# First feed-forward layer of a cross-attention block by seven block products, and its output projection on f16 halves

## The chip, the cores and the metric
One Trainium2 chip, one of its cores. The metric is the device time of one execution in microseconds (us). The core has five engines with queues in program order: TensorE (PE, with its weight loads PEld), VectorE (DVE), ScalarE (ACT), GpSimd (POOL) and SyncE (SP), which issues the DMAs. They wait for each other by semaphores.

## The reference, cut to what matters
16 sequences of 512 rows and 512 features, 16 heads, 2048 hidden features.
```python
q, k, v = (split_heads(t @ W + b) for t, W, b in ((x, Wq, bq), (ctx, Wk, bk), (ctx, Wv, bv)))
attn = softmax(where(j < i, q @ k.T / sqrt(32), -1e30)); attn[row 0] = 0
x = layer_norm(x + (attn @ v) @ Wo + bo, g1, be1)
out = layer_norm(x + relu(x @ W1 + b1) @ W2 + b2, g2, be2)
```

## The kernel before, in words
Every product is made in halves: a number is split into a high and a low half (f16, or f32r in the projection), and three matmuls (high high, high low, low high) stand for one of f32.

`attention` runs 16 sequences in windows of 48 slots. Beside it, `Bounds` scans W2 and then W1 for their largest entries, one tile of 128x1024 in each sequence; for W2 (sequences 0 to 7) GpSimd also makes five sums of quarters, and three DMAs store seven blocks, so that the second layer needs seven block products instead of eight.

`feed` takes over at the end of the attention: 32 chunks of 256 tokens in windows of 16 slots. It is interleaved with the attention's last slots (`side_by_side`), up to about its slot 20. `due(window, s, ..., first, span)` gives the item whose step `first` falls in this slot: a chunk's steps are spread over some 48 slots, and three chunks overlap. Each engine's program goes through the slots in order; within one slot the order is that of the text. No barrier stands between slots: only semaphores hold the engines together. Slot numbers of the steady state are taken modulo 16.

A chunk's steps in `feed`: the context and x are loaded (`LOAD`), the context is turned in 32x32 blocks on DVE (`OTR`), split into halves (`turned`), multiplied by Wo (`PROJ`, slots 5 and 6, two PSUM banks `front`), added to x and normed (`RES`, `NORM1`), stored and loaded turned (`x1_rows`, `X1_TURN` 13), split (`x1_halves`). The first layer (`FFN1` 16, one block of 128 hidden features a slot) writes `h_ps`, ScalarE makes `hf` of it, GpSimd sums, ScalarE and DVE the halves `hs`. The second layer (`FFN2` 22, two slots for one pair) adds seven products in `acc`, four PSUM banks, which the next chunk needs one slot after the last product. DVE reads them out in slots `RES2 - 1` (four parts) and `RES2` (two), then norms (`STATS2`, `NORM2`). Weight chunks go through `raw`: ScalarE makes the high half, DVE the low half, 44 chunks and Wo's four.

## Time and profile before
| | us |
|---|---|
| median of three runs (2651.48 to 2652.87) | 2652.14 |
| profiled execution, its own time | 2651.14 |
| its span, first to last instruction | 2649.3 |
| TensorE busy (94%) | 2498.2 |
| VectorE busy (80%) | 2116.9 |
| ScalarE busy (62%) | 1629.8 |
| GpSimd busy (60%) | 1585.5 |

The granted TensorE clock is 0.989 of full speed over the span. Busy shares are means over the attention (to some 1120 us), the handover and the feed-forward part, whose limits differ; they are read by stage. A matmul's own duration holds its way through the pipeline, so what it costs in a stream is read from start to start.

### The profile page before, as it was taken

To read this page: it belongs to the slowest core of one execution; us is meant where nothing else is said; L and a number is where in the kernel's file an instruction comes from. 1 tells how busy PE (TensorE), PEld (TensorE's weight loads), DVE (VectorE), ACT (ScalarE), POOL (GpSimd) and SP (SyncE) were. 2 spreads that over 40 slices of the span, in tenths; PEclk is the share of its full clock that TensorE was granted. 3 is DMA by queue.
4 is the path that set the end of the run, shared out by engine and by line. 5 is a ranking of instruction groups with operands and counts; after the bars stand their busy time and mean duration, and the time that the engine had idled before them with its cause. 6 is when DMAs were issued, how large, how long until landed. Compare 5 with 4: busy or idle time off the path is not lost.

```text
span 2649.3 us, 62863 instructions
## 1 busy us (share of the span) xinstructions
PE 2498.2 (94%) x22664; PEld 1873.3 (71%) x22664; DVE 2116.9 (80%) x4886; ACT 1629.8 (62%) x2881; POOL 1585.5 (60%) x1721
## 2 busy tenths in 40 slices
PE   4899999999999999879999999999999999999998
PEld 1455555555555555557888888888888888888887
DVE  7999999999999999878767777767767676767675
ACT  2788889899899999886344444343444343444433
POOL 2677777777777777666455555555555555554543
PEclk9999999999999999989999999999999999999999
DMA  5344444443344443345232313222222222222220
GB/s 169 110 117 117 119 114 110 115 109 103 92 103 105 106 106 97 89 140 159 53 69 50 71 46 67 50 69 53 66 56 61 61 57 64 57 65 57 65 57 25
DMA packets 444456, 225.04 MB, mean 85 GB/s; under 512 B 302368, under 2 KB 388192, under 8 KB 444144
## 3 DMA queue, kind: packets, MB, share of 16 engines
q1 hardware_dynamic: 442544, 219.71, 32.5%
q8 instruction: 179, 2.93, 0.5%
q10 hardware_dynamic: 1600, 1.31, 0.2%
q14 instruction: 133, 1.09, 0.1%
HBM read 112.36 MB, written 57.69 MB: 64 GB/s over the span
## 4 chain that ended last, share of the span: by engine, by line
PE 63%; DVE 8%; SPq 8%; POOL 8%; issue 7%; DMA 4%; ACT 1%; ACTq 0%; DVEq 0%; POOLq 0%
PE h_ps L1646 23%; PE acc L1662 20%; POOL prob_lo L495 7%; PE front L1632 6%; PE lin_ps L934 5%; SPq L421 4%; PE max_ps L907 2%; PE st_ps L955 2%; DVE max_ps L886 2%; PE lin_ps L930 1%; PE o_ps L973 1%; SPq L458 1%; SPq L1065 1%; DMA heads<-stage 1%; PE st_ps L986 1%
## 5 line engine op out<-in xcount | busy, mean ns | idle before, releaser
L495 POOL TENSOR_TENSOR prob_lo<-probs,prob_hi 128x512 f16<-128x512 f32 (+1 forms) x768 | 797.8, 1047 | 335.2 <-ACT prob_hi L582 318.5
L1646 PE MATMUL h_ps<-x_halves,W 128*128 128x256 f16 x6144 | 756.2, 273 | 1.8 <-ACT hf L1431 1.7
L1662 PE MATMUL acc<-W,hs 128*128 128x256 f16 x5376 | 669.6, 273 | 0.3 <-DVE hs L1599 0.3
L1646 PEld LDWEIGHTS h_ps<-x_halves,W 128*128 128x128 f16 x6144 | 596.5, 98 | 87.5 <-issue 14.8
L1431 ACT ACTIVATE hf<-h_ps,b1s,scale_evac 128x256 f32<-128x256 f32 x512 | 284.9, 563 | 559.7 <-PE h_ps L1646 557.2
L1662 PEld LDWEIGHTS acc<-W,hs 128*128 128x128 f16 x5376 | 526.0, 98 | 61.4 <-DVE hs L1599 0.6
L1356 POOL TENSOR_TENSOR hf<-hf 128x256 f32<-128x256 f32 x256 | 243.4, 951 | 483.1 <-ACT hf L1431 482.7
L588 ACT ACTIVATE probs<-st_ps,exp_scale 128x512 f32<-128x512 f32 (+1 forms) x768 | 469.3, 611 | 98.2 <-PE st_ps L986 91.6
L886 DVE CUSTOM_DVE_ANT_0 max_ps<-max_ps,mask_q 128x256 f32<-128x256 f32 (+2 forms) x768 | 418.2, 560 | 47.1 <-PE max_ps L907 43.4
L582 ACT ACTIVATE prob_hi<-probs 128x512 f16<-128x512 f32 (+1 forms) x768 | 427.9, 557 | 23.0 <-issue 7.3
L1599 DVE TENSOR_TENSOR hs<-hf,hs 128x896 f16<-128x896 f32 x256 | 282.0, 1121 | 147.8 <-ACT hs L1420 147.7
L1420 ACT ACTIVATE hs<-hf 128x896 f16<-128x896 f32 x256 | 242.0, 945 | 252.8 <-POOL hf L1359 248.4
L907 PE MATMUL max_ps<-heads 96*128 96x128 f16 (+3 forms) x1024 | 258.1, 303 | 74.9 <-DVE maxima L886 62.9
L955 PE MATMUL st_ps<-heads 98*128 98x512 f16 (+3 forms) x1024 | 268.4, 303 | 14.3 <-DMA heads<-rows 11.0
L973 PE MATMUL o_ps<-V,prob_hi 128*128 128x65 f16 x2560 | 247.6, 191 | 9.5 <-DVE onorm L807 4.7
L907 PEld LDWEIGHTS max_ps<-heads 96*128 96x128 f16 x1024 | 89.8, 97 | 231.0 <-DVE maxima L886 100.5
L975 PE MATMUL o_ps<-V,prob_lo 128*128 128x33 f16 x2560 | 237.6, 179 | 0.0
L973 PEld LDWEIGHTS o_ps<-V,prob_hi 128*128 128x128 f16 x2560 | 200.5, 97 | 51.0 <-issue 10.4
L930 PE MATMUL lin_ps<-wv,acts 128*128 128x512 f16 x768 | 209.5, 383 | 26.9 <-DVE acts L596 26.8
L1357 POOL TENSOR_TENSOR hf<-hf 128x256 f32<-128x256 f32 x256 | 229.3, 896 | 0.0
L934 PE MATMUL lin_ps<-acts,wk 128*128 128x512 f16 x768 | 208.6, 381 | 5.4 <-DVE V L853 5.4
L934 PE MATMUL lin_ps<-acts,wq 128*128 128x512 f16 x768 | 207.6, 380 | 3.2 <-DVE V L853 3.2
(152 smaller groups left out, 3526.1 us busy)
## 6 DMA issues: line engine op xcount, KB each, us to landing
heads<-stage SPq DMA_DIRECT2D x748, 64.0 KB, 2.1
raw_c<-in_cT SPq DMA_DIRECT2D x64, 256.0 KB, 3.4
raw_x<-in_xT SPq DMA_DIRECT2D x64, 256.0 KB, 4.4
o_in<-ctx_rows SPq DMA_DIRECT2D x256, 64.0 KB, 2.5
x_in<-in_x SPq DMA_DIRECT2D x32, 512.0 KB, 4.0
x_rows<-x SPq DMA_DIRECT2D x64, 256.0 KB, 2.1
o_in<-x_rows SPq DMA_DIRECT2D x256, 64.0 KB, 2.4
out<-y SPq DMA_DIRECT2D x32, 512.0 KB, 3.0
```

What stands on the lines that cost most here:

```text
L495: pool.tensor_tensor(prob_lo[:, k % 4, 0:w], probs[:, k % PROBS, 0:w], prob_hi[:, k % 4, 0:w], ALU.subtract).then_inc(pl_done, 1)
L582: act.activation(prob_hi[:, k % 4, 0:w], probs[:, k % PROBS, 0:w], ACT.Copy).then_inc(ph_done, 1)
L588: act.activation(probs[:, k % PROBS, 0:w], st_ps[:, k % 2, 0:w], ACT.Exp, bias=PROB_BIAS, scale=exp_scale[:, at:at + 1]).then_inc(exp_done, 1)
L886: last = dve.tensor_tensor_reduce(out=scores[:, a, :], in0=scores[:, a, :], in1=mask_q[:, S - w:S], scale=1.0, scalar=MASKED, op0=ALU.add, ...
L907: last = pe.matmul(max_ps[:, bank, a * w:(a + 1) * w], heads[t][0:96, 0, i, q * P:(q + 1) * P], heads[t][0:96, 1, i, 0:w], start=(a == 0), ...
L934: last = pe.matmul(lin_ps[:, n % 2, :], W[kind][:, aw, j, t * P:(t + 1) * P], act_part(item, side, aa)[:, j, :], start=(j == 0 and m == 0) ...
L955: pe.matmul(st_ps[:, k % 2, at:at + w], heads[t][0:98, 1, i, kt * P:(kt + 1) * P], heads[t][0:98, 0, i, kt * P:S], start=(m == 0), stop=False,
L973: pe.matmul(o[:, 0:2 * HD + 1], prob_hi[:, k % 4, col:col + P], v[:, 0:2 * HD + 1], start=(k % 3 == 0 and q == 0), stop=False, skip_group_ ...
L1431: act.activation(to, h_ps[:, f % 2, 0:T].rearrange("p (u n) -> p u n", u=U), ACT.Relu, bias=b1s[:, f:f + 1], scale=h_evac).then_inc(h_out, 1)
L1599: dve.tensor_tensor(hs[:, p % HS, 1, :, :], hf[:, (PAIRS * item.n + p) % HF, 1:1 + PRODUCTS, :], hs[:, p % HS, 0, :, :], ALU.subtract).the ...
L1646: last = pe.matmul(h_ps[:, f % 2, 0:T], W1[:, aw, j, f * P:(f + 1) * P], x1_halves[:, item.parity, aa, j, :], start=(j == 0 and m == 0), s ...
L1662: last = pe.matmul(acc_products[:, n, :], hs[:, p % HS, aa, n, :], W2[:, p, aw, n, :], start=(p == 0 and m == 0 and n % 2 == 0), stop=(p = ...
```

## The change
The first layer is done for four blocks of hidden features (two pairs) at a time, in four stages with seven products together. x1 and W1 are cut in quarters; W1's sums are made by GpSimd in sequences 8 to 15, as W2's were before them, and stored to `mixed_w1`; x1's sums are made by GpSimd in each chunk (`X1_MIX`), after which ScalarE and DVE split seven blocks of x1 instead of four. Partial sums stay in PSUM (`mix_b`, `mix_ad`) and are drawn out between the stages: ScalarE copies M2 and U2 to `sums`, DVE adds C11, C22 and C21, ScalarE applies the ReLU. `first_product` waits for C11 before stage 1, for U2 before stage 2 and for C22 before stage 3.

`FFN1` goes to slot 18, `FFN2` to 30 (14 in the window), `PROJ` to slots 4 and 6 with one PSUM bank, so that the second projection waits for the first residual; `RES2 - 1`, `RES2` and `STATS2` fall on slots 13, 14 and 15. x1 is loaded back into `y` from DRAM instead of being kept. Wo and the context are split into f16 halves; Wo is loaded and scanned early in the attention (`load_wo`). W1 now has 28 chunks, so there are 56 of W1 and W2, and Wo's four. The order within a slot on ScalarE is: last quadrant (`C12_AT`), ReLUs, x1 high halves, context high half, weights, roots, `H_HI`, M2, U2; on DVE: C11, C22, C21, x1 low halves, turns, context low half, residual and first norm, reads of `acc`, second norm, `H_LO`, weights.

```diff
+        quarter = scan[:, 0:2, :].rearrange("p i (j e n) -> p (i j) e n", j=2, e=2)
+        a11, a12, a21, a22 = (quarter[:, 2 * i:2 * i + 2, e, :] for e, i in ((0, 0), (0, 1), (1, 0), (1, 1)))
+        s1, s2, s4 = (scan[:, 2 + n // 2, 256 * (n % 2):256 * (n % 2) + 256].rearrange("p (j n) -> p j n", j=2)
+                      for n in range(3))
+        return [(s1, a21, ALU.add, a22), (s2, s1, ALU.subtract, a11), (s4, a12, ALU.subtract, s2),
+                (a21, a11, ALU.subtract, a21)]
...
-                    for n, src in enumerate(bounds.tiles(item.n)):
+                    for n, (dst, src) in enumerate(bounds.tiles(item.n, scan)):
                         wait_for(sp, bounds.kept, 1, item, 0)
-                        if item.n <= bounds.pairs:
-                            wait_for(sp, bounds.mix_stored, 48, item, 0)
-                        sp.dma_start(scan[:, n, :], src).then_inc(bounds.loaded[n], 16)
+                        wait_for(sp, bounds.mix_stored, 48, item, 0)
+                        sp.dma_start(dst, src).then_inc(bounds.loaded[n], 16)
                 for item, _ in due(window, s, SLOTS, B, MIX_STORE):
...
+                for n in range(5):
                     for item, _ in due(window, s, SLOTS, B, MIX + 3 * n):
-                        if item.n >= bounds.pairs:
+                        mixes = bounds.mixes(item.n, scan)
+                        if n >= len(mixes):
                             continue
...
+                        if item.n >= bounds.pairs and n:
+                            pool.wait_ge(bounds.mixed, bounds.mixed_by(item.n) + n)
+                        elif n >= 3:
+                            pool.wait_ge(bounds.mixed, bounds.mixed_by(item.n) + 3)
+                        out, in0, op, in1 = mixes[n]
+                        pool.tensor_tensor(out, in0, in1, op).then_inc(bounds.mixed, 1)
...
+    BV_AT = 3
     OTR = 2
+    ADD_BO = 3
+    PROJ = (4, 6)
+    RES = (5, 7)
     NORM1 = 8
     X1_TURN = 13
+    X1_MIX = (X1_TURN + 2, X1_TURN + 4)
+    X1_HI = (X1_TURN + 3, X1_TURN + 5)
+    X1_LO = (X1_TURN + 4, X1_TURN + 6)
+    FFN1 = 18
+    STAGES = (0, 2, 3, 5)
+    M2_AT = FFN1
+    C11_AT, U2_AT, C22_AT, C21_AT, C12_AT = FFN1 + 1, FFN1 + 2, FFN1 + 4, FFN1 + 6, FFN1 + 6
+    RELU = FFN1 + 7
+    MIX = FFN1 + 8
+    H_HI = FFN1 + 9
+    H_LO = FFN1 + 10
+    FFN2 = FFN1 + 12
+    Y_LOAD = 40
+    ADD_B2 = 43
     RES2 = FFN2 + FT
+    STATS2 = RES2 + 1
     NORM2 = RES2 + 8
     STORE = RES2 + 9
+    SPLIT = 4
     RAW = early.RAW
     PAIRS = FT // 2
+    TWOS = PAIRS // 2
     PRODUCTS = 7
     HALVES = ((0, 1, 2, 3), (4, 5, 6))
+    STEPS = ((("b", 1, 1), ("a", 0, 0), ("d", 2, 2)), (("a", 5, 5),), (("a", 4, 4),), (("a", 6, 3), ("d", 3, 6)))
...
+    def region(name, two):
+
+
+        if name == "b":
+            return mix_b[:, 0:2, :]
+        return mix_ad[:, two % 2, {"a": 0, "d": 2}[name]:{"a": 2, "d": 4}[name], :]
...
+                for half in range(2):
+                    for item in x1_items(window, s, X1_MIX[half]):
+                        for n, (to, in0, in1) in enumerate((((4, 2, 0), (2, 3, 2)), ((5, 3, 4), (6, 1, 5)))[half]):
+                            if (half, n) == (0, 0):
+                                wait_for(pool, x1_turned, U, item, U)
+                                wait_for(pool, x1_lo, 2, item, 0)
+                                pool.wait_ge(bv_done, 1)
+                            else:
+                                wait_for(pool, x1_mixed, 4, item, 2 * half + n)
+                            pool.tensor_tensor(blocks[:, to, :], blocks[:, in0, :], blocks[:, in1, :], ALU.subtract
+                                               ).then_inc(x1_mixed, 1)
...
+                for item, k in when(window, s, C12_AT, FT):
+                    two, r = k // 4, k % 4
+                    if r < 2:
+                        p = 2 * two + r
...
+                        wait_for(act, c21_done, TWOS, item, two + 1)
+                        wait_for(act, h_lo, PAIRS, item, p + 1 - HF)
+                        act.activation(hf[:, (PAIRS * item.n + p) % HF, 8, :], region("a", two)[:, r, :], ACT.Relu,
+                                       bias=b1s[:, 2 * p:2 * p + 1], scale=h_evac).then_inc(h_last, 1)
+                for item, k in when(window, s, RELU, FT):
+                    two, r = k // 4, k % 4
+                    if r < 2:
+                        p = 2 * two + r
+                        h, c = hf[:, (PAIRS * item.n + p) % HF, :, :], sums[:, two % 2, r, :, :]
+                        wait_for(act, c21_done, TWOS, item, two + 1)
+                        wait_for(act, c22_done, TWOS, item, two + 1)
+                        for to, odd in ((slice(2, 3), 0), (slice(0, 2), 1)):
+                            act.activation(h[:, to, :], c[:, to, :], ACT.Relu, bias=b1s[:, 2 * p + odd:2 * p + odd + 1],
+                                           scale=h_evac).then_inc(h_out, 1)
+                for half in range(2):
+                    for item in x1_items(window, s, X1_HI[half]):
+                        part = X1_PARTS[half]
+                        wait_for(act, x1_mixed, 4, item, 2 * half + 2)
+
+                        wait_for(act, stage_done[3], TWOS, item, -TWOS)
+                        act.activation(x1_halves[:, item.parity, 0, part, :, :],
+                                       blocks[:, part, :].rearrange("p m (j n) -> p m j n", j=2), ACT.Copy,
+                                       scale=scale_x1).then_inc(x1_hi, 1)
...
+                for item, k in when(window, s, M2_AT, FT):
+                    if k % 4 == 0:
+                        two = k // 4
...
+                        wait_for(act, m2_done, TWOS, item, two + 1)
+                        wait_for(act, h_out, FT, item, 4 * two - 4)
+                        act.activation(sums[:, two % 2, :, 2, :], region("b", two), ACT.Copy).then_inc(m2_kept, 1)
+                for item, k in when(window, s, U2_AT, FT):
+                    if k % 4 == 0:
+                        two = k // 4
+                        wait_for(act, stage_done[1], TWOS, item, two + 1)
+                        act.activation(sums[:, two % 2, :, 0:2, :].rearrange("p r c n -> p c r n"),
+                                       mix_ad[:, two % 2, :, :].rearrange("p (c r) n -> p c r n", c=2), ACT.Copy
+                                       ).then_inc(u2_kept, 1)
...
+                for item, k in when(window, s, C11_AT, FT):
+                    if k % 4 == 0:
+                        two = k // 4
+                        wait_for(dve, stage_done[0], TWOS, item, two + 1)
+                        wait_for(dve, m2_kept, TWOS, item, two + 1)
+                        dve.tensor_tensor(sums[:, two % 2, :, 2, :], sums[:, two % 2, :, 2, :], region("a", two), ALU.add
+                                          ).then_inc(c11_done, 1)
+                for item, k in when(window, s, C22_AT, FT):
+                    if k % 4 == 0:
+                        two = k // 4
+                        wait_for(dve, stage_done[2], TWOS, item, two + 1)
+                        wait_for(dve, u2_kept, TWOS, item, two + 1)
+                        dve.tensor_tensor(sums[:, two % 2, :, 1, :], sums[:, two % 2, :, 1, :], region("a", two), ALU.add
+                                          ).then_inc(c22_done, 1)
+                for item, k in when(window, s, C21_AT, FT):
+                    if k % 4 == 0:
+                        two = k // 4
+                        wait_for(dve, stage_done[3], TWOS, item, two + 1)
+                        dve.tensor_tensor(sums[:, two % 2, :, 0, :], sums[:, two % 2, :, 0, :], region("d", two), ALU.add
+                                          ).then_inc(c21_done, 1)
...
-                        dve.scalar_tensor_tensor(out=tile, in0=front[:, u, :],
+                        dve.scalar_tensor_tensor(out=tile, in0=front[:, :],
...
+        def first_product(item, two, stage):
+
+            if stage == 0:
+                wait_for(pe, x1_lo, 2, item, 1)
...
+                wait_for(pe, h_last, PAIRS, item, 2 * two + 2 - 4)
+                wait_for(pe, c21_done, TWOS, item, two + 1 - 2)
+                wait_for(pe, m2_kept, TWOS, item, two)
+            elif stage == 1:
+                wait_for(pe, x1_lo, 2, item, 2)
+                wait_for(pe, c11_done, TWOS, item, two + 1)
+            elif stage == 2:
+                wait_for(pe, u2_kept, TWOS, item, two + 1)
+            else:
+                wait_for(pe, c22_done, TWOS, item, two + 1)
+            for name, at_w, at_x in STEPS[stage]:
+                for r in range(2):
+                    for j in range(2):
+                        for m, (aw, aa) in enumerate(((0, 0), (0, 1), (1, 0))):
+                            opens = stage == 0 and name != "d" and r == 0 and j == 0 and m == 0
+                            last = pe.matmul(region(name, two)[:, r, :], w1_of(2 * two + r, aw, at_w)[:, j, :],
+                                             x1_halves[:, item.parity, aa, at_x, j, :], start=opens,
+                                             stop=(j == 1 and m == 2), skip_group_check=True)
+                if name == "b":
+                    last.then_inc(m2_done, 1)
+            last.then_inc(stage_done[stage], 1)
...
+        def first_products(window, s):
+
+            for stage, at in enumerate(STAGES):
+                for item, k in when(window, s, FFN1 + at, FT):
+                    if k % 4 == 0:
+                        first_product(item, k // 4, stage)
...
+                    for item, _ in when(window, s, PROJ[u]):
+                        wait_for(pe, ctx_lo, U, item, u + 1)
+                        wait_for(pe, res_done, U, item, u)
                         if item.n == 0:
-                            pe.wait_ge(w_lo, KT)
+                            pe.wait_ge(wo_lo, KT)
+                            pe.wait_ge(*before.lin_read)
                         for j in range(KT):
                             for m, (aa, aw) in enumerate(((0, 0), (0, 1), (1, 0))):
-                                last = pe.matmul(front[:, u, :], turned[:, item.parity, aa, j, u * P:(u + 1) * P],
+                                last = pe.matmul(front[:, :], turned[:, item.parity, aa, j, u * P:(u + 1) * P],
                                                  Wo[:, aw, j, :], start=(j == 0 and m == 0),
...
+                if s % 2 == 0:
+                    first_products(window, s)
+                    second_products(window, s)
+                else:
+                    second_products(window, s)
+                    first_products(window, s)
```

## Rows read from the trace of the kernel before

**Rows 1.** Busy time by stage: us, PE, PEld, DVE, ACT, POOL, clock, DMA.
```profile
1209.00:1257.00 48.00, 44.43 (x370) 38.05 (x369) 43.01 (x56) 31.98 (x52) 29.22 (x29) 0.96 0.53 143
1257.00:2557.60 1300.60, 1300.23 (x11130) 1142.39 (x11129) 924.03 (x1508) 535.23 (x870) 674.30 (x811) 1.00 0.26 60
2557.60:2634.00 76.40, 76.40 (x675) 67.70 (x674) 48.52 (x77) 32.04 (x51) 34.89 (x50) 1.00 0.10 29
```

**Rows 2.** Order of time, TensorE: the projections of chunks 2 and 31.
```profile
1256.95 3.01 PE L1632 MATMUL front<-Wo,turned 128*128 128x512 f32 x12
...
2558.41 2.99 PE L1632 MATMUL front<-Wo,turned 128*128 128x512 f32 x12
```

**Rows 3.** Order of time, a steady chunk: start, us, instructions.
```profile
1808.74 1.47 PE L1646 MATMUL h_ps<-x_halves,W 128*128 128x256 f16 x12
...
1810.05 1.47 PE L1662 MATMUL acc<-W,hs 128*128 128x256 f16 x12
```

**Rows 4.** The same: a projection and what follows it.
```profile
1800.96 3.02 PE L1632 MATMUL front<-Wo,turned 128*128 128x512 f32 x12
...
1803.82 1.21 PEld L1646 LDWEIGHTS h_ps<-x_halves,W 128*128 128x128 f16 x12 [0.26 <-issue]
```

**Rows 5.** Order of time in the attention, TensorE.
```profile
800.22 0.38 PE L907 MATMUL max_ps<-heads 96*128 96x128 f16 x4 [1.03 <-DVE maxima L886]
800.44 0.38 PE L911 MATMUL max_ps<-mask_q,identb 128*128 128x512 bf16 x1
...
800.99 0.19 PE L973 MATMUL o_ps<-V,prob_hi 128*128 128x65 f16 x1
...
801.21 0.81 PE L934 MATMUL lin_ps<-acts,wq 128*128 128x512 f16 x3
801.86 0.38 PE L907 MATMUL max_ps<-heads 96*128 96x256 f16 x2
```

**Rows 6.** SP's queue: a DMA issued once in a sequence.
```profile
121.93 0.58 SPq L433 DMA_DIRECT2D top_rows<-top  x1
...
542.82 0.58 SPq L433 DMA_DIRECT2D top_rows<-top  x1
...
1018.29 0.58 SPq L433 DMA_DIRECT2D top_rows<-top  x1
```

**Rows 7.** Groups by shape, 1664 to 2561 us: busy, mean ns, idle before.
```profile
L1431 ACT ACTIVATE hf<-h_ps,b1s,scale_evac 128x256 f32<-128x256 f32 x320 | 178.0, 563 | 364.0 <-PE h_ps L1646 361.6 <-DVE hs L1599 2.0
L1599 DVE TENSOR_TENSOR hs<-hf,hs 128x896 f16<-128x896 f32 x161 | 175.6, 1110 | 93.2 <-ACT hs L1420 93.2
...
L1357 POOL TENSOR_TENSOR hf<-hf 128x256 f32<-128x256 f32 x161 | 142.0, 882 | 0.0
...
L1519 DVE SCALAR_TENSOR_TENSOR x_halves<-block_turned,scale,x_halves 128x512 f16<-128x512 f32 x40 | 33.6, 839 | 53.1 <-ACT x_halves L1383 53.1
...
L1540 DVE SCALAR_TENSOR_TENSOR x<-front,value_scale,x_in 128x512 f32<-128x512 f32 x40 | 29.7, 743 | 0.0
```

**Rows 8.** Groups by shape, whole execution.
```profile
L1420 ACT ACTIVATE hs<-hf 128x896 f16<-128x896 f32 x256 | 242.0, 945 | 252.8 <-POOL hf L1359 248.4 <-PE acc L1662 0.7
...
L582 ACT ACTIVATE prob_hi<-probs 128x256 f16<-128x256 f32 x256 | 105.6, 412 | 3.3
...
L807 DVE TENSOR_TENSOR onorm<-osum,o_ps 128x128 f32<-128x128 f32 x256 | 71.0, 277 | 0.1
...
L1603 DVE SCALAR_TENSOR_TENSOR W<-raw,scale,W 128x512 f16<-128x512 f32 x44 | 42.8, 1006 | 4.0 <-ACT W L1408 4.0
```

**Rows 9.** Order of time, DVE, around a chunk's end.
```profile
1800.15 1.40 DVE L1567 SCALAR_TENSOR_TENSOR y<-acc,scale_evac,x 128x512 f32<-128x512 f32 x2
...
1802.91 0.74 DVE L1540 SCALAR_TENSOR_TENSOR x<-front,value_scale,x_in 128x512 f32<-128x512 f32 x1
...
1814.11 1.28 DVE L1443 BATCH_NORM_STATS2 stats<-y 128x6 f32<-128x512 f32 x2
...
1817.16 2.08 DVE L1599 TENSOR_TENSOR hs<-hf,hs 128x896 f16<-128x896 f32 x2
```

More of the change, by code:

```diff
@@ L56 @@
 SUM_TOP = 8192.0
+MIX_TOP = 4096.0
 BACK = 2
+FEED_BACK = 3
 class Item:
@@ L64, in __init__, with due @@
         self.n, self.parity = n, n % 2
-def due(window, slot, slots, items, first, span=1):
-    for back in range(BACK + 1):
+def due(window, slot, slots, items, first, span=1, behind=BACK):
+    for back in range(behind + 1):
         k = slot + slots * back - first
@@ L138, in __init__, with tiles @@
         self.ready = sem("scales_ready")
-    def tiles(self, step):
-        w, k = (self.w2, step) if step < self.pairs else (self.w1, step - self.pairs)
-        return [w[(2 * k + n) * P:(2 * k + n + 1) * P, :] for n in (1, 0)]
+    def tiles(self, step, scan):
+        if step < self.pairs:
+            return [(scan[:, n, :], self.w2[(2 * step + 1 - n) * P:(2 * step + 2 - n) * P, :]) for n in range(2)]
+        k = step - self.pairs
+        return [(scan[:, n, :].rearrange("p (j c) -> p j c", j=2),
+                 self.w1[2 * n * P:2 * (n + 1) * P, 256 * k:256 * (k + 1)].rearrange("(j p) c -> p j c", p=P))
+                for n in range(2)]
@@ L425, in sync @@
                         sp.wait_ge(stored[i], 32 * GROUPS // 2)
+                    sp.wait_ge(bounds.kept, B + 1)
+                    sp.wait_ge(bounds.mix_stored, 48 * bounds.pairs + 48)
                     load_first(sp)
@@ L700, in scales @@
         def scales(dve):
-            w1, w2, b1, norm = (bounds.top[:, n:n + 1] for n in range(4))
+            w1, w2, b1, norm, wo = (bounds.top[:, n:n + 1] for n in range(5))
             value, power, scale, evac = bounds.value, bounds.power, bounds.scale, bounds.evac
@@ L1016, in attention @@
     programs.o_read = (o_out, HEADS * B)
+    programs.scans_stored = (bounds.mix_stored, 48 * B)
+    programs.rows_stored = [(stored[i], 32 * GROUPS // 2 * B) for i in range(2)]
     return programs
@@ new lines, in feed @@
+    w1_at = weight_chunks(bounds.mixed_w1, (W1a, W1b))
+    w2_at = weight_chunks(bounds.mixed_w2, (W2a, W2b))
+    order = [(w, n) for w, two in (("w1", 0), ("w1", 1), ("w2", 0), ("w1", 2), ("w2", 1), ("w1", 3), ("w2", 2), ("w2", 3))
+             for n in range(PRODUCTS * two, PRODUCTS * (two + 1))]
+    chunks = [{"w1": w1_at, "w2": w2_at}[w][n] for w, n in order]
+    scale_w1, scale_w2, scale_x1, scale_h, scale_wo = (bounds.scale[:, n:n + 1] for n in range(5))
+    weight_scale = [{"w1": scale_w1, "w2": scale_w2}[w] for w, _ in order]
@@ new lines, in chunks_of, with over, w1_of @@
+    def chunks_of(w, two):
+        return order.index((w, PRODUCTS * (two + 1) - 1)) + 1
+    def w2_chunks(p):
+        return order.index(("w2", (PRODUCTS * (p + 1) - 1) // 2)) + 1
+    def over(n):
+        w, c = order[n]
+        if w == "w1":
+            return []
+        if c < PRODUCTS:
+            return before.outputs_staged
+        return [before.scans_stored, *before.heads_read, before.probs_read]
+    def w1_of(p, part, n):
+        half = (W1a, W1b)[p // TWOS]
+        return half[:, p % TWOS, part, n, :].rearrange("p (j f) -> p j f", j=2)
@@ L1362, in scalar @@
     def scalar(act):
-        for n in range(KT):
-            act.wait_ge(raw_loaded[n], 16)
-            act.activation(part_of(n, 0), raw_slot(n), ACT.Copy).then_inc(w_hi, 1)
+        for j in range(KT):
+            act.wait_ge(bounds.wo_loaded, 16 * KT)
+            act.wait_ge(bounds.ready, 2)
+            act.activation(Wo[:, 0, j, :], early.wo_raw[:, j, :], ACT.Copy, scale=scale_wo).then_inc(wo_hi, 1)
             yield
@@ L1403, in scalar @@
                         act.wait_ge(*before.inputs_read)
+                        act.wait_ge(*before.splits_done)
                         act.wait_ge(bounds.ready, 2)
-                    if n >= KT and order[n - KT][0] == "w2":
-                        for done in over_w2(order[n - KT][1]):
-                            act.wait_ge(*done)
-                    act.activation(part_of(n, 0), raw_of(n), ACT.Copy, scale=weight_scale[n]).then_inc(w_hi, 1)
-                for item, _ in due(window, s, SLOTS, CHUNKS, NORM1):
+                    for done in over(n):
+                        act.wait_ge(*done)
```

592 lines of the change are left out of this document (303 added, 289 removed).

## The prediction
> **What bounds the kernel now.** I read the views in this order: busy time by stage, then one steady chunk (256 tokens) in order of time, then the attention. From 1257 us to 2557.6 us TensorE is busy 1300.23 of 1300.60 us; DVE has 924, ScalarE 535, GpSimd 674 [rows 1]. In this stretch only matmul time counts. Its period is that of the output projection: from 1256.95 to 2558.41 us lie 29 chunks, 44.88 us each [rows 2]. It is made of matmuls: a group of 12 with 256 columns takes 1.31 us start to start, 109 ns each [rows 3]; 12 of the projection (512 columns, f32r) take 2.86 us, 238 ns each [rows 4]. A chunk has 192 of the first layer (21.0 us), 168 of the second (18.3) and 24 of the projection (5.7): 45.0, so there is no idle. The attention is not bound by one engine; the period of a sequence can be read from a DMA issued once in each [rows 6].
>
> **First layer: 336 matmuls of 128 columns for 192 of 256.** Seven products x 2 x 2 x 3 = 84 for four blocks, 336 in a chunk: 7/8 of the columns, but twice the instructions for the same columns. Four of 128 columns took 0.22 us, 55 ns each, each with its own weights [rows 5]. So 336 x 55 ns = 18.5 us, 2.5 us less than 21.0. Can the weight loads keep up? Eight matmuls of 65 and 33 columns, each with its own load, ran in 0.22 us [rows 5]: a load needs at most 27.5 ns and fits behind 55.
>
> The Trainium skill, "TensorE: Matmul & The Clock Gate", section "Back-to-back issue gap", speaks against this: a long stream of load and matmul pairs is put there at about 81 ns for 128 columns. By it the first layer would be 336 x 81 ns = 27.2 us, and the change would lose 6.2 us a chunk there instead of gaining 2.5. The row says 55, but over four matmuls only.
>
> **Projection on f16 halves.** Three f16 matmuls of 512 columns take 0.65 us, 217 ns each [rows 5], for 238: 24 x 21 ns = 0.5 us less. TensorE's floor is then 18.5 + 18.3 + 5.2 = 42.0 us; with a few joints, 42.2, against 44.9: 2.7 us a chunk, if nothing else shows.
>
> **What is added beside it.** The sums go step by step through PSUM, and TensorE now waits for other engines inside the first layer: per four blocks (4 slots) for C11 and C22 (DVE) and for U2 (ScalarE).
> - DVE: three additions of 256 elements out of PSUM. 128 elements took 277 ns, 512 took 743 [rows 7, 8]: interpolated 0.41 us. Twelve are 4.9 us a chunk; the low halves of seven blocks instead of four cost some 0.5 more. From 924/29 = 31.9 us a chunk it goes to 37.3.
> - ScalarE: 256 elements took 412 ns, 896 took 945 [rows 7, 8], so 0.83 us per 1000; 128 give 0.31, 512 give 0.63. Bias and scale read from tiles, and PSUM, add some 0.1 to 0.15 (563 ns for 256 [rows 7]). I take 0.45 for the last quadrant, 0.9 for the two other ReLUs, 0.62 for U2, 1.15 for four x1 blocks (1024 elements). It ends near 27 us a chunk.
> - GpSimd: four subtractions of 256 elements more, 0.9 us each [rows 7]: 3.5 us, off the path.
>
> No engine is full. But DVE's work comes in lumps, its queue is in order, and so is ScalarE's. So I walk a steady chunk slot by slot. TensorE's slot lasts, by its number modulo 4: 2: stage 0 (36 x 55 = 2.0) + four products 1.31 = 3.3; 3: three products 0.98 + stage 3 1.3 = 2.3; 0: stage 1 0.66 + 1.31 = 2.0; 1: 0.98 + 0.66 = 1.65; slots 4 and 6 have 2.6 of projection more.
>
> Slots 13 to 1, TensorE at slot 13 = 0. In slot 13 DVE turns an x1 half (0.71) and reads four parts of the finished accumulator: its last matmul is at 0, the four take 2.8 [rows 9], done at 3.3. Slot 14: C22 0.4, turn 0.7, two more parts 1.5: 5.9. TensorE reaches the first use of those banks (slot 15) at 4.9 and waits until 6.0: **stall A, 1.0**. In before the accumulator changes hands in slots 5 and 6, behind both projections (5.7 us); now they are at 4 and 6, and no projection stands there. DVE goes on: low half of h 1.1 to 7.0, C11 to 7.4, the second norm's statistics and centring, 3.05 us [rows 9], to 10.5, then C21 to 10.95. ScalarE's last-quadrant ReLU of slot 0 waits for C21, and behind it in its queue stand four x1 blocks and U2: 0.45 + 1.15 + 0.62 gives 13.3. TensorE wants U2 for stage 2 at 11.3 (it has had stall A): **stall B, 2.0**. A and B together do not depend on how they are split: 13.3 against 10.25.
>
> Slots 2 to 6, slot 2 = 0. ScalarE is still behind (ReLUs, x1 blocks, M2 kept at 3.85), so C11, low x1 half and low ctx half on DVE end at 6.2; the projection of slot 4 is due at 5.6: **stall C, 0.6**. From stage 1's end in slot 4: U2 0.7, slot 5's ReLUs 1.35, high ctx half 0.63, low half on DVE 0.9 (839 ns for a like one [rows 7]), residual 0.75, since there is now one `front` bank: 4.4 us to the second projection. TensorE has 1.31 + 0.98 + 0.66 = 2.95 to do: **stall D, 1.45**. In slots 7 to 12 the same walk gives none: DVE passes C21 of slot 8 some 0.5 us before it hurts.
>
> Sum: 42.2 + 1.0 + 2.0 + 0.6 + 1.5 = 47.3 us a chunk, 2.4 more than now. With A+B at 2.4, C at 0, D at 1.3 it is 46; with GpSimd slowing DVE's lumps by a tenth (+1.2) 48.5.
>
> **The attention.** W1's sums take the place of the plain look in sequences 8 to 15: four additions and three stores in each, SP waiting for them before the next load. Before has this already for W2 in sequences 0 to 7: from 121.93 to 542.82 us six periods, 70.15 us each; from there to 1018.29 seven, 67.92 [rows 6]. So 2.2 us a sequence for five additions; four or five fifths of it, eight times: 14 to 18, taken as 16. The early load of Wo, its scan and its two halves replace like work.
>
> **Beginning and end.** There are 56 weight chunks of 1.0 us each on DVE [rows 8] for 44 and Wo's four, which stay. Three more come before slot 21, +3. Between 1209 us (slot 21) and 1257 (slot 37) DVE is busy 43.0 of 48 us [rows 1]; it gets six chunks (6), the additions (4.9), 0.5: +11. Slot 37 comes at 1257 + 16 + 3 + 11 = 1287. At the end TensorE had 76.4 us to do and then a tail of 15.3 (2634 to the end of the span) [rows 1]. Now the second layer lags six slots more (6 x 1.15 = 6.9) and the first two (2.3), less 3.5 for the cheaper matmuls, plus two stalls A+B and one D (7.5): 89.6.
>
> **Sum.** 1287 + 29 x 47.3 + 89.6 + 15.3 = 2763.6 us of span. The profiled execution took 2651.14 for a span of 2649.30 (+1.8), the median of three is 2652.14: 2765 us. Cycles of 46 and 48.5 give 2728 and 2800.
>
> **Rivals.**
> - *Covered.* The bursts on DVE don't reach TensorE: the stretch before U2 in slot 0 (13.3) would have to shrink under 10.25, and the way to the second projection (4.4) under 2.95. It decides at a cycle of 43.5, above which nothing is gained over the whole kernel. Price: 1287 + 29 x 42.2 + 82 + 15.3 + 1.8 = 2610. For it: DVE is idle 5 us a chunk, some small durations are guessed. Against: two chains in series, both long by a third. 0.16.
> - *Half covered.* Only one of the two remains, a cycle of 44.7: 2687. 0.13.
> - *Weights not hidden.* In a long run of 128 columns the 27.5 ns of a load add to each 55: 9.2 us a chunk; B is then covered and some 2 us of the stalls remain, cycle 53.5, 2950 in the end. Against: the eight pairs of rows 5. This is also the case in which the change does not give the 7/8 that it is to give. 0.06. The page's 81 ns would mean this rival.
> - *A draw*, the stalls just eating the gain: 0.03.
>
> **How the numbers follow.** Forecast 0.60 (2715 to 2815), 0.02 left beyond it. A run can tell about 0.2% from no change. Faster 0.17, same 0.03, slower 0.80. The range has to reach the covered case and the slow end: 2610 to 2825, leaving out half of covered, the weights and the rest.
>
> **What would show it.** First-layer matmuls at 55 ns start to start; 336 of them. Idle on TensorE near 5 us a chunk, put down to U2's copy on ScalarE, to the residual or low ctx half on DVE, and to the accumulator's read-out; idle at 0 would mean covered. The projection 47.3 us apart. The DMA of rows 6 some 70 us apart in all sequences. I would be wrong if the small ScalarE instructions take less than 0.3 us, if the sums move in the queues other than walked, or if matmuls with many loads run slower than in rows 5.

## The result and the profile after

The changed kernel takes 2840.49 us (median, 2836.57 to 2843.02), the one before beside it 2652.51: a ratio of 1.0706, interval 1.0688 to 1.0725. Slower, as forecast, but by 188 us instead of 113, and above the range's upper end of 2825. The profiled execution has a span of 2834.8 us for 2649.3.

First by stage (us, busy time and instructions of PE, PEld, DVE, ACT, POOL, then granted clock, DMA share, GB/s); it answers [rows 1]:

```profile
1216.00:1278.00 62.00, 41.75 (x463) 36.24 (x463) 47.35 (x74) 38.77 (x68) 27.54 (x27) 0.83 0.56 157
1278.00:2720.00 1442.00, 1279.81 (x15316) 1110.95 (x15317) 1114.36 (x1859) 693.21 (x1338) 816.43 (x929) 0.98 0.26 65
2720.00:2800.00 80.00, 74.20 (x950) 66.79 (x949) 56.99 (x98) 40.76 (x80) 39.54 (x51) 1.00 0.14 41
2800.00:2835.00 35.00, 17.55 (x153) 14.47 (x150) 19.39 (x33) 8.94 (x17) 11.39 (x14) 0.76 0.13 46
```

TensorE, which had no idle time in the steady stretch before, now has 162 us of it there, and its granted clock is 0.98 for 1.00. Then the projections of chunks 2 and 31, which answer [rows 2], and the DMA of [rows 6] (start, duration):

```profile
1278.17 4.02 PE L1875 MATMUL front<-Wo,turned 128*128 128x512 f16 x10 [2.35 <-DVE turned L1716]
...
2719.27 2.75 PE L1875 MATMUL front<-Wo,turned 128*128 128x512 f16 x12
```

```profile
121.71 0.58 SPq L477 DMA_DIRECT2D top_rows<-top  x1
...
540.92 0.58 SPq L477 DMA_DIRECT2D top_rows<-top  x1
609.15 0.58 SPq L477 DMA_DIRECT2D top_rows<-top  x1
```

The same DMA comes last at 1021.69 us (1018.29 before). These marks split the 185.5 us of span (2834.8 less 2649.3): up to chunk 2, +21.2 (of it the attention +3.4); 29 cycles of 49.69 us instead of 44.88, +139.6; from chunk 31 to the end 115.5 instead of 90.9, +24.6. Three quarters are in the cycle, and what stands in it is in TensorE's table of waits, 1330 to 2720 us, 28 chunks (us in total, times, longest):

```profile
PE mix_ad L1821 <- ACT h_sums L1591: 61.7, 28, 2.2
PE mix_b L1821 <- issue: 36.7, 28, 1.5
PE front L1875 <- DVE x L1728: 31.1, 28, 1.1
PE acc L1849 <- DVE raw L1770: 19.8, 28, 0.7
PE front L1875 <- DVE turned L1716: 7.4, 13, 0.6
```

Five waits, each once in a chunk (C in 13 of 28). Four have the prediction's letters: B (stage 2 waits for the U2 copy), D (second projection waits for the residual), A (accumulator read-out), C (first projection waits for the context's low half). The second line is new; I call it **E**. "issue" says only that the profile shows no releaser. One chunk in order of time shows where they stand:

```profile
1924.77 2.76 PE L1875 MATMUL front<-Wo,turned 128*128 128x512 f16 x12 [0.56 <-DVE turned L1716]
...
1930.33 0.83 PE L1821 MATMUL mix_ad<-x_halves,W1a 128*128 128x128 f16 x12
1932.28 2.75 PE L1875 MATMUL front<-Wo,turned 128*128 128x512 f16 x12 [1.11 <-DVE x L1728]
...
1943.47 0.83 PE L1821 MATMUL mix_ad<-x_halves,W1a 128*128 128x128 f16 x12
1945.60 0.83 PE L1821 MATMUL mix_b<-x_halves,W1b 128*128 128x128 f16 x12 [1.30 <-issue]
1946.27 1.50 PE L1821 MATMUL mix_ad<-x_halves,W1b 128*128 128x128 f16 x24
1947.61 2.46 PE L1849 MATMUL acc<-W2b,hs 128*128 128x256 f16 x21
...
1956.88 1.47 PE L1849 MATMUL acc<-W2a,hs 128*128 128x256 f16 x12
1959.07 1.16 PE L1849 MATMUL acc<-W2a,hs 128*128 128x256 f16 x9 [0.71 <-DVE raw L1770]
...
1962.07 2.46 PE L1849 MATMUL acc<-W2a,hs 128*128 128x256 f16 x21
1966.73 0.84 PE L1821 MATMUL mix_ad<-x_halves,W1b 128*128 128x128 f16 x12 [2.20 <-ACT h_sums L1591]
1967.56 1.08 PE L1821 MATMUL mix_b<-x_halves,W1a 128*128 128x128 f16 x12
1968.43 2.77 PE L1821 MATMUL mix_ad<-x_halves,W1a 128*128 128x128 f16 x24
1970.99 2.68 PE L1849 MATMUL acc<-W2a,hs 128*128 128x256 f16 x21
```

Read it from start to start. 24 first-layer matmuls take 1946.27 to 1947.61, 1.34 us: 56 ns each. Twelve take 0.67, so behind the twelve of 1943.47 the next could start at 1944.14; it starts at 1945.60: E costs 1.46 us, a little more than the printed 1.30. In the same way A costs 0.88, B 2.37, D 1.28, and C 0.73 where it occurs. And behind B the same 24 matmuls take 2.56 us (1968.43 to 1970.99), 107 ns each: there the clock has fallen from 2.4 to 1.2 GHz. The 12, 12, 24 and 21 matmuls behind B take 1.8 us more than at the full clock. This happens in every other chunk, and the cycles alternate (first projections at 1924.77, 1974.84 and 2024.00): 49.2 us without it and 50.1 with it, since C is then missing.

The chain behind B, on VectorE and ScalarE, is the predicted one: statistics and centring of the second norm (L1605 to L1620), then C21 (L1668), then the ReLU and the x1 blocks on ScalarE, then the U2 copy (L1591). Stage 2 starts at 1966.73.

```profile
1960.40 1.27 DVE L1605 BATCH_NORM_STATS2 stats<-raw 128x6 f32<-128x512 f32 x2
...
1964.25 0.41 DVE L1668 TENSOR_TENSOR h_sums<-h_sums,mix_ad 128x256 f32<-128x256 f32 x1
...
1966.09 0.58 ACT L1591 ACTIVATE h_sums<-mix_ad 128x512 f32<-128x512 f32 x1
```

The chain behind E (the bracket gives the idle time before an instruction, and its releaser):

```profile
1939.34 1.41 DVE L1620 SCALAR_TENSOR_TENSOR x<-x,mv,vec_g 128x512 f32<-128x512 f32 x2
1940.71 0.42 DVE L1668 TENSOR_TENSOR h_sums<-h_sums,mix_ad 128x256 f32<-128x256 f32 x1
...
1942.54 1.42 DVE L1643 SCALAR_TENSOR_TENSOR x<-x,rs,vec_be 128x512 f32<-128x512 f32 x2
1943.87 1.08 DVE L1786 TENSOR_TENSOR hs<-hf,hs 128x896 f16<-128x896 f32 x1
...
1945.05 0.46 ACT L1523 ACTIVATE hf<-mix_ad,b1s,scale_evac 128x128 f32<-128x128 f32 x1 [2.85 <-DVE hs L1786]
```

The low halves of a pair (L1786) are last in VectorE's slot, behind the first normalisation. They free one of the three `hf` tiles. ScalarE's ReLU of the last quadrant (L1523) waits 2.85 us for that tile, and stage 0 of the next four blocks, which writes over that quadrant, waits for the ReLU, which starts at 1945.05 and takes 0.46: matmuls at 1945.60.

### The profile page after: what moved, and what is told of

Read it like the earlier page. It is cut to its first block, busy times and chain, and to the rows that moved or that the text cites. A ratio compares the mean times of both kernels' runs of the same rounds, so it can differ in the third digit from the quotient of the medians.

```text
span 2834.8 us, 74428 instructions
## 1 busy us (share of the span) xinstructions
PE 2481.1 (88%) x27268; PEld 1837.3 (65%) x27268; DVE 2332.5 (82%) x5286; ACT 1809.9 (64%) x3405; POOL 1760.1 (62%) x1881
## 4 chain that ended last, share of the span: by engine, by line
PE 44%; DVE 23%; issue 12%; SPq 6%; ACT 6%; POOL 5%; DMA 3%; ACTq 0%; DVEq 0%; POOLq 0%
PE mix_ad L1821 11%; PE acc L1849 9%; PE front L1875 6%; PE lin_ps L988 5%; POOL prob_lo L539 5%; SPq L463 3%; DVE hs L1786 3%; PE mix_b L1821 2%; PE max_ps L961 2%; DVE max_ps L940 2%; PE st_ps L1009 2%; DVE raw L1620 2%; ACT hf L1533 2%; PE lin_ps L984 1%; DVE raw L1754 1%
## 5 line engine op out<-in xcount | busy, mean ns | idle before, releaser
L1849 PE MATMUL acc<-W2a,hs 128*128 128x256 f16 x4032 | 480.5, 274 | 26.4 <-DVE raw L1770 21.2
L1523 ACT ACTIVATE hf<-mix_ad,b1s,scale_evac 128x128 f32<-128x128 f32 x256 | 116.8, 456 | 602.3 <-DVE h_sums L1668 499.0
L1849 PEld LDWEIGHTS acc<-W2a,hs 128*128 128x128 f16 x4032 | 386.2, 98 | 77.5 <-DVE raw L1770 29.6
L1786 DVE TENSOR_TENSOR hs<-hf,hs 128x896 f16<-128x896 f32 x256 | 327.4, 1280 | 63.4 <-ACT hs L1576 61.0
L1821 PE MATMUL mix_ad<-x_halves,W1b 128*128 128x128 f16 x4608 | 297.7, 220 | 68.1 <-ACT h_sums L1591 68.1
L1821 PEld LDWEIGHTS mix_ad<-x_halves,W1b 128*128 128x128 f16 x4608 | 272.3, 99 | 79.4 <-ACT h_sums L1591 77.2
L1821 PE MATMUL mix_ad<-x_halves,W1a 128*128 128x128 f16 x4608 | 313.2, 227 | 9.7 <-ACT h_sums L1591 7.2
L1821 PEld LDWEIGHTS mix_ad<-x_halves,W1a 128*128 128x128 f16 x4608 | 292.5, 102 | 20.5 <-ACT h_sums L1591 7.6
L1533 ACT ACTIVATE hf<-h_sums,b1s,scale_evac 128x128 f32<-128x128 f32 (+1 forms) x512 | 249.8, 538 | 0.0
```

What stands on the lines that cost most here:

```text
L1533: act.activation(h[:, to, :], c[:, to, :], ACT.Relu, bias=b1s[:, 2 * p + odd:2 * p + odd + 1], scale=h_evac).then_inc(h_out, 1)
L1786: dve.tensor_tensor(hs[p % HS][:, 1, :, :], hf[:, (PAIRS * item.n + p) % HF, 1:1 + PRODUCTS, :], hs[p % HS][:, 0, :, :], ALU.subtract).the ...
L1821: last = pe.matmul(region(name, two)[:, r, :], w1_of(2 * two + r, aw, at_w)[:, j, :], x1_halves[:, item.parity, aa, at_x, j, :], start=ope ...
L1849: last = pe.matmul(acc_products[:, n, :], hs[p % HS][:, aa, n, :], w2_of(p, aw, n), start=(p == 0 and m == 0 and n % 2 == 0), stop=(p == P ...
```

## The experiments

Experiment 1 starts from the kernel before, all others from the changed kernel. Experiments 2 to 10 only reorder work; experiment 11 adds some. The ratio is to the kernel before, measured beside it (2653 to 2655 us).

**1. One part alone.** In the kernel before, float16 for the projection's operands, at their old addresses:

```diff
-        Wo = sb("Wo", [P, 2, KT, D], F32R)
+        Wo = sb("Wo", [P, 2, KT, D], F16)
+        skip("rest_of_Wo", 8192)
...
-        turned = sb("turned", [P, 2, 2, KT, T], F32R)
+        turned = sb("turned", [P, 2, 2, KT, T], F16)
+        skip("rest_of_turned", 8192)
```

> The kernel before with one part of the change alone: the output projection's weights, the context halves and with them the 12 products of bv with Wo are float16 pairs instead of float32r pairs, all at their old addresses; block sums and first layer as before. Theory: TensorE is busy 1300 of 1300.6 us in the steady part, so what it saves is saved: a projection of 12 matmuls took 2.86 us in float32r and 2.60 us in float16 (kernel after), so 0.26 us times 64 projections is 16.6 us: 2655 falls to 2638 us (0.994). Rival: something else ends just behind TensorE (VectorE has 924 of 1300 us) and takes up half or all of it: 2646 to 2655 us.

2644.11 us, ratio 0.9967 [0.9957, 0.9977]: a gain of 10 us: less than the 17 of the theory, and a little more than the 0 to 9 of the rival. Its cycle, in order of time:

```profile
1798.46 2.75 PE L1634 MATMUL front<-Wo,turned 128*128 128x512 f16 x12
1801.05 1.47 PE L1648 MATMUL h_ps<-x_halves,W 128*128 128x256 f16 x12
1802.36 1.15 PE L1664 MATMUL acc<-W,hs 128*128 128x256 f16 x9
1803.34 2.75 PE L1634 MATMUL front<-Wo,turned 128*128 128x512 f16 x12
...
1842.94 2.75 PE L1634 MATMUL front<-Wo,turned 128*128 128x512 f16 x12
```

Twelve matmuls take 2.59 us, as expected (2.86 in float32r, [rows 4]). But the nine of 256 columns ahead of the second projection take 0.98 us where they took 0.90 before (1800.06 to 1800.96 there), so 0.08 of the 0.27 us is lost again at this joint. This cycle is 44.48 us, 0.4 shorter; the mean of 29 is 44.53, and together they are 10 us shorter, as much as the median gained. (Chunk 2 comes 6 us later in this profile, which is open.) The rival's reason is not what is seen: from 1257 to 2550 us TensorE waits for another engine once, 1.2 us.

**2. Stall B: the statistics of the second normalisation five slots later.**

```diff
-    STATS2 = RES2 + 1
+    STATS2 = RES2 + 6
```

> The changed kernel with one number changed: the second norm's statistics and centring on DVE (3.05 us) go from slot 15 to slot 4, where DVE waits for ScalarE anyway. Theory (waits in series in queues kept in order): C21 of slot 0 comes some 3 us earlier, so TensorE's 2.2 us wait for U2's copy falls under 0.3 us and with it the stretch of half clock behind it; the chunk period goes from 49.7 to about 46.4 us, the whole from 2840 to about 2745 us. Rival (DVE's total work or the small matmuls bound the chunk): the same work is done, so the period stays at 49.7 us and the whole within 5 us of 2840.

2793.17 us, ratio 1.0516 [1.0499, 1.0534]. The longest of TensorE's waits, 29 chunks:

```profile
PE front L1875 <- DVE x L1728: 63.5, 29, 2.5
PE mix_b L1821 <- issue: 38.0, 29, 1.5
PE acc L1849 <- DVE raw L1770: 20.6, 29, 0.7
```

B is gone, the clock is 1.00. But D went from 1.1 to 2.2: the statistics now stand ahead of a low half (L1786, at 1912.31) for which ScalarE's ReLU waits until 1913.49, and the context's high half stands behind that ReLU. The mean of the 29 cycles is 47.9 us where 46.4 was expected; 1.1 of the missing 1.5 us is D's growth.

**3. Stall E: the low halves ahead of the residual and the normalisations.** The block of L1786 is moved, nothing else.

```diff
+                for item, k in when(window, s, H_LO, FT):
+                    ...
                 for u in range(U):
                     for item, _ in when(window, s, RES[u]):
```

> The changed kernel with DVE's low halves of h (H_LO) taken ahead of the residual and the norms within a slot. In slot 9 ScalarE's last-quadrant ReLU waits for a low half made behind the first norm of slot 8, and stage 0 of slot 10 waits for that ReLU: TensorE idle 1.3 to 1.46 us, put down to issue. Theory: this wait goes, period 49.7 to 48.3 us, whole 2840 to about 2800 us. If that idle has another cause (a wait for x1, or the instruction stream of TensorE itself): no change, 2840 us.

2777.65 us, ratio 1.0461 [1.0440, 1.0482], more than expected:

```profile
PE acc L1849 <- DVE raw L1776: 42.8, 29, 2.3
PE front L1875 <- DVE x L1734: 32.2, 29, 1.1
PE mix_ad L1821 <- ACT h_sums L1591: 31.0, 28, 1.1
PE front L1875 <- DVE turned L1716: 16.6, 29, 0.6
```

E is gone, which confirms its chain. B fell to 1.1 as A rose to 1.5, and the clock stayed at 1.00, which I had not foreseen; the mean cycle is 47.4 us where 48.3 was expected.

**4. Stall A: the read-outs of the accumulator ahead of the turns.**

```diff
+                for item, _ in when(window, s, RES2 - 1):
+                    ...
+                for item, _ in when(window, s, RES2):
+                    ...
                 for half in range(2):
                     for item in x1_items(window, s, X1_LO[half]):
```

> The changed kernel with DVE's reads of the finished accumulator taken ahead of the x1 low halves and the turns within a slot. Theory as in the prediction (the accumulator's wait A and the wait B for U2 are one chain on DVE and only split between them): A falls from 0.7 us to under 0.1 and B grows by as much, the whole stays within 8 us of 2840. Rival (every wait stands for itself): A goes and B stays, 29 periods 0.8 us shorter, 2817 us.

2844.19 us, ratio 1.0712 [1.0691, 1.0733]. A fell from 19.8 to 9.7 us in 28 chunks (to 0.35 each, not under 0.1), B rose from 61.7 to 74.3; their sum went from 81.5 to 84.0. A and B are one budget.

**5. Stall D: on ScalarE the context's high halves ahead of the ReLUs.**

```diff
+                for u in range(U):
+                    for item, _ in when(window, s, OTR + 1 + 2 * u):
+                        ...
                 for item, k in when(window, s, RELU, FT):
```

> The changed kernel with ScalarE's high half of the context taken ahead of the ReLUs of the same slot. Theory: the way from stage 1 to the second projection gets 0.97 us shorter, TensorE's wait for the residual falls from 1.11 us to about 0.2, period 49.7 to 48.8 us, whole 2840 to about 2814 us. Rival (TensorE is late by total work of the others): 2840 us.

2825.66 us, ratio 1.0642 [1.0621, 1.0663]. D is down to 0.2 us; E rose from 36.7 to 54.0 us and took back some half of the gain. Seen from the start of the second projection, the low half that E waits for starts 12.2 us later (1927.62 to 1939.83), where it was 11.6 (1932.28 to 1943.87). That this comes from the ReLUs, which now stand behind, is argued and not shown.

**6. Stall B by ScalarE's order: the U2 copy ahead of the last-quadrant ReLU.**

```diff
+                for item, k in when(window, s, U2_AT, FT):
+                    ...
                 for item, k in when(window, s, C12_AT, FT):
```

> The changed kernel, and on ScalarE the copy of the two U2 regions ahead of the ReLUs of the last quadrant in its slot. Theory: the 2.2 us wait of stage 2 for this copy comes from VectorE (C21 behind the statistics, which the ReLUs wait for), and the copy stands behind those ReLUs on ScalarE only by its order. Moved ahead, the copy is in time, stage 2's wait goes, and the delayed C21 is then met one stage on, where the next pair's stage 0 waits for the same C21 and for the last quadrant: so the same 2 us is lost under another name and the time stays within 15 us of 2840. Rival: the copy's place on ScalarE was all of it, and 29 times 2.37 us go with the clock drop behind it (0.9 us a cycle): 2745 us.

2885.44 us in a single run, 45 more than the changed kernel. The longest waits, 25 chunks:

```profile
PE mix_b L1821 <- DVE x_halves L1692: 59.2, 25, 2.4
PE mix_b L1821 <- issue: 50.2, 25, 2.2
PE front L1875 <- DVE x L1728: 36.4, 25, 1.5
```

The wait for U2 is gone and the same 2.4 us stand one stage later, at the next pair's stage 0, as the theory said. The profile puts them down to the low halves of x1 (L1692), though, and not to C21 or the last quadrant. That E and D would grow too (to 2.0 and 1.5), the theory did not say. The time was to stay within 15 us and is 45 longer.

**7. The edits of 2 and 3 together.**

> The two moves that helped most, together: VectorE's statistics of the second normalisation five slots later, and the subtraction that makes the low halves of the block sums ahead of the residual and the normalisations. Theory (stalls are single waits in VectorE's order, so moves add up, except where one had made the other's): the statistics no longer hold C21 (2.37 us of a cycle go), the low halves no longer stand behind the normalisations nor behind the statistics (1.30 go), the projection's wait is back at 1.1 to 1.3 instead of the 2.2 that it was with the late statistics alone. Against the version with the low halves first (2778 us, a cycle of 47.5 us, of it 1.1 us waiting for the U2 copy) this leaves 46.4 us a cycle, and 29 cycles make 2745 us. Rival: a removed stall is taken up by the next wait in the same chain, the cycle stays at 47.5 us and the time at 2770 or above. A third case, that VectorE's total work in the chain is the bound, would also keep 2770.

2727.09 us, ratio 1.0281 [1.0261, 1.0301]: 50 us better than move 3 alone, where 33 were expected. B and E are gone, A is 1.44, D 1.11, C 0.48. Alone, move 2 had given 47 us and move 3 63: the sum is 110 and the pair gave 113, so the two do add up. The mean cycle is 45.9 us, so the rival (the next wait takes it) and the third case (VectorE's total work), both at 47.5 and 2770, are refuted for this pair.

**8. The edits of 2, 3 and 5.**

> Late statistics, low halves first, and ScalarE's context halves ahead of the ReLUs (the version at 2709 us without its read-outs first). The pair without the context move took 2727 us, with waits a cycle of 1.44 us (accumulator), 0.48 (context's low half) and 1.11 (residual). Theory (the context move takes the last two away, as it took the residual's away when made alone): 1.6 us of 29 cycles go, 2727 falls to 2681 us, which is below the version at 2709, whose read-outs first cost more than they gave. Rival: the ReLUs behind the context halves delay the block sums' chain as in the version with the context move alone (where the wait of stage 0 grew from 1.3 to 2.0 us), the gain is eaten, 2715 us or more.

2706.75 us, ratio 1.0205 [1.0188, 1.0222]: a gain of 20 us where 46 were expected, and yet below the rival's 2715. D is down to 0.2 and its loss no longer appears as E, but C stayed and A rose from 1.44 to 1.70; the cycle is 45.08 us.

**9. The edits of 2, 3, 4 and 5.**

> Four moves together: late statistics, low halves first, the read-outs of the second layer's accumulator ahead of the turns and x1's low halves on VectorE, and the context's high halves ahead of the ReLUs on ScalarE. Theory (the waits are separate): against the pair (expected 2745 us) the accumulator wait of 0.7 to 1.5 us a cycle shrinks to 0.3 and the residual wait of 1.1 us goes, which is 1.9 to 2.3 us of 29 cycles, or 2680 to 2690 us, still 1 per cent above the kernel before (2652), since the bare work of TensorE is 42.2 us a cycle and the rest of the time is a longer start and a longer end. Rival: read-outs first and context first each lengthened the other waits when made alone (2844 and 2826 us instead of gains of 20 and 37), so that they give nothing here either: 2745 us or more.

2708.67 us, ratio 1.0210 [1.0188, 1.0233], between the theory and its rival, and the same as experiment 8: the read-outs first gave nothing. Against experiment 8, A fell to 0.34, and C rose to 1.25 in this chunk and to 1.57 in the mean:

```profile
1950.40 1.16 PE L1849 MATMUL acc<-W2a,hs 128*128 128x256 f16 x9 [0.34 <-DVE raw L1709]
...
1963.83 2.76 PE L1875 MATMUL front<-Wo,turned 128*128 128x512 f16 x12 [1.25 <-DVE turned L1740]
```

The turns of x1, now behind the read-outs, delay GpSimd's block differences, and the context is turned into the same tile: VectorE waits 1.61 us for it (released by GpSimd, L1480). The loss travels through a shared buffer.

**10. Experiment 9 with the projections, their residuals and the first normalisation one slot later.**

```diff
-    PROJ = (4, 6)
-    RES = (5, 7)
-    NORM1 = 8
+    PROJ = (5, 7)
+    RES = (6, 8)
+    NORM1 = 9
```

(The idle matmuls of slot 8 in the first chunk, which would write the same bank, are left out.)

> The four moves of the version at 2709 us, and the projections, their residuals and the first normalisation one slot later (5, 7; 6, 8; 9). What that version still waits for in a cycle of 45.25 us is 1.25 us until the context's low half (first projection), 0.34 until an accumulator read-out, 0.24 until x1's low half and 0.23 until the residual. Theory (each wait is a matter of the slot in which the producer stands on VectorE): the first wait goes, the residual's may grow to at most its old 1.1, so a cycle of 44.0 to 44.9 us and 2672 to 2700 us, 2672 if nothing else grows. Rival: the later normalisation makes x1 late, the wait for x1's low half grows by what the projection gained, and the time stays at 2709 or above. By neither does it come below the kernel before (2654): the matmuls' own 42.3 to 43 us a cycle, a start 21 us and an end 25 us longer leave no room.

2814.73 us, ratio 1.0599 [1.0568, 1.0631]: 106 us longer than experiment 9. The rival's side is right (2709 or above), but not its reason. C is gone, and a wait of 3.4 us for C22 (VectorE) stands in its place, which neither had named; the wait for x1's low half grew too, but only to 11.0 us in 16 of 26 chunks.

```profile
1946.11 0.41 DVE L1662 TENSOR_TENSOR h_sums<-h_sums,mix_ad 128x256 f32<-128x256 f32 x1
1946.58 1.51 PE L1821 MATMUL mix_ad<-x_halves,W1a 128*128 128x128 f16 x24 [3.42 <-DVE h_sums L1662]
```

In VectorE's order the residual and the first normalisation stand directly ahead of C22 here, from 1936.59 to 1946.11 without a break. Some of their instructions are longer than in the changed kernel (L1633 takes 1.19 us for 0.16, L1643 2.04 for 1.42). Why they are longer was not tested, and no run moved C22 ahead of them.

**11. The clock: work in the idle stretch of B, no wait shortened.** Eight matmuls whose result nobody reads:

```diff
                     second_products(window, s)
+                    if s == 1 and 2 <= window < CHUNKS:
+                        pe.wait_ge(res_done, U * window)
+                        for _ in range(8):
+                            pe.matmul(front[:, :], Wo[:, 0, 0, 0:P], Wo[:, 0, 0, :], start=True, stop=True)
                     first_products(window, s)
```

> The changed kernel, and in slot 1 of a chunk, between the second layer's matmuls and the wait of stage 2 for the U2 copy, eight matmuls of 512 columns into the free bank of the projection, whose result nobody reads: 8 times 0.22 us are 1.8 us of work in an idle stretch of 2.2 to 2.4 us. Theory (the granted clock falls behind this idle stretch, in every other chunk, and that costs 0.9 us there net): the clock is 1.00 in the steady part, every cycle takes the 49.2 us of those without a fall, and 2840 becomes 2825 us, the first of these moves that gains without shortening any wait. Rival 1: the clock falls for another reason (the mean activity of the whole cycle), 2840. Rival 2: the filler is longer than the idle stretch left at its place and delays stage 2, over 2845.

2830.26 us, ratio 1.0667 [1.0647, 1.0687], some 10 us below the changed kernel (1.0706). The trace decides: the clock is 1.00 from 1330 to 2720 us, and every cycle is 49.2 us:

```profile
2614.15 2.76 PE L1875 MATMUL front<-Wo,turned 128*128 128x512 f16 x12 [0.58 <-DVE turned L1716]
...
2663.32 2.76 PE L1875 MATMUL front<-Wo,turned 128*128 128x512 f16 x12 [0.57 <-DVE turned L1716]
...
2702.89 1.89 PE L1887 MATMUL front<-Wo 128*128 128x512 f16 x8
2712.48 2.76 PE L1875 MATMUL front<-Wo,turned 128*128 128x512 f16 x12 [0.57 <-DVE turned L1716]
```

The idle stretch left before stage 2 is 0.48 us. So with work in that stretch the clock does not fall, and rival 2 (a delay) is refuted. Rival 1 is not: the eight matmuls also raised TensorE's busy share from 1330 to 2580 us from 0.89 to 0.92, and no run separates the stretch from the activity of the whole cycle. The 29 cycles are 13 us shorter in all; chunk 2 comes 6 us later here, which is open.

## Why the prediction was right and wrong

- *Direction and mechanism: right.* TensorE's matmul time fell and waits inside the first layer cost more than that. Stalls A to D stand at the named instructions and engines, and B is gone when the statistics move (experiment 2).
- *First layer at 55 ns: right*, 56 ns over 24 and 36 matmuls. "Weights not hidden" is refuted. The 81 ns of the Trainium skill ("TensorE: Matmul & The Clock Gate", "Back-to-back issue gap") are not what this trace shows.
- *Projection 0.5 us less: 0.35 in the mean of 29 cycles* (experiment 1).
- *Floor 42.2:* the cycle of 49.69 less the measured stalls and the clock's cost below is 42.5.
- *Load of the other engines:* VectorE 38.3 us a chunk (1073.3 in 28), predicted 37.3; ScalarE 23.8 (667.0 in 28), predicted near 27. The 0.41 us for an addition is what was measured, but the two rows give 0.43 when interpolated.
- *A + B = 3.0: measured 0.88 + 2.37 = 3.25*, and experiment 4 shows that they are one budget, as written.
- *C = 0.6: 0.73, but only in chunks without a fallen clock, 0.34 in the mean. D = 1.45: 1.28.*
- ***"In slots 7 to 12 the same walk gives none": this step failed.*** E, 1.46 us, stands there, 29 times: 42 us. The walk followed C21 and the sums, where VectorE was indeed in time. It left out the other thing that VectorE owes in that slot, the low halves last in its queue and through them the ring of three `hf` tiles. Experiment 3 took E away by moving these halves.
- *The clock was taken as 1.00.* It costs 0.9 us a cycle in the mean, some 26 us. Without the fall C comes in every chunk, so the net cost is less: in experiment 11 the 29 cycles are 13 us shorter, the whole time 10. The stalls of the sum had a second price that the sum did not have.
- *The term that was mis-sized is the cycle: 47.3, measured 49.69.* 29 times the 2.39 are 69 of the 71 us by which the span was missed (2834.8 for 2763.6).
- *Attention +16: measured +3.4.* Seven periods with W1's sums are 68.7 us each (540.92 to 1021.69) for 67.92 without; 0.8 more and not 2.2. GpSimd makes four such additions in a sequence there (24 in six) and five in those before (25 in five), so the additions are fewer by a fifth, and the extra time by nearly two thirds. The rest of the difference is open.
- *Beginning:* without the attention +17.8 to the first projection of chunk 2, predicted +14. But the sum counts from slot 37, where the projection stood before, and the changed kernel has it in slot 36. Slot 37 starts near 1284.4 in chunk 2 and near 2723.8 in chunk 31 (behind the stage and the twelve products that follow the projection), so that by the sum's own mark the beginning is +24. The clock is 0.83 there, for 0.96 before; what else makes it longer is open.
- *End:* from that slot 111 us, predicted 104.9. From chunk 31 on TensorE waits for nobody in the kernel before; now it waits 10.8 us, for which the sum had 7.5. The longest wait was not in the walk:

```profile
2813.51 4.61 PE L1849 MATMUL acc<-W2a,hs 128*128 128x256 f16 x21 [5.16 <-DVE hs L1786]
```

Again low halves of h stand behind a normalisation on VectorE (L1643, at 2811.04), and the 21 matmuls take 4.45 us instead of 2.29. No run took this wait away.

- *That attention, beginning and end together are missed by only some 3 us* is luck: -12.6, +10 and +6 nearly cancel.
- *"Covered" at 2610:* its price was too low, by what the runs show. Experiment 8 has a cycle of 45.08, and chunk 31 comes at 2591.12, 32.7 us later than before, and the end takes 22 us more. With its 2.2 us of waits gone it would take 2707 - 29 x 2.2 = 2643 us by this estimate, a gain of 0.4%. No version that ran beats the kernel before except the float16 projection alone (2644).

## What to carry to other kernels

Here a product cut into stages that pass through PSUM turned a stream that never waited into one with four or five waits a chunk. Price such a change by walking every consumer of the loaded engine's queue, the last in the slot and the rings that it frees among them, not only the chain of the new data. Move the lumps (statistics, low halves) away from where an engine answers TensorE: two such moves gave back 113 of 188 us here. Stalls that share an engine's order or a buffer are one budget: moving one block alone often only renames the wait.

## What the runs showed of the hardware

- The granted clock of TensorE fell from 2.4 to 1.2 GHz after an idle stretch of 2.2 to 2.4 us that stood 5 us behind one of 0.7, in every other chunk; with 1.8 us of matmuls in that stretch it never did (experiment 11). The length alone does not decide: in experiment 2, D was 2.2 us, behind an idle stretch of 0.3, and the clock stayed at 1.00. What else decides stays open.
- 128-column float16 matmuls, each with its own weights, run at 56 ns over streams of 36.
- Twelve float16 matmuls of 512 columns take 0.27 us less than in float32r (2.59 for 2.86), but 0.08 us of that is lost at the one joint that was read.
